# Source and destination rows handled apart, look-ups two groups ahead, codes loaded first

## The reference

```python
def gat_layer(x, W, attn_l, attn_r, bias, src, dst, num_nodes):
    feat = (x @ W).reshape(num_nodes, H, D)
    el = jnp.sum(feat * attn_l[None], axis=-1)
    er = jnp.sum(feat * attn_r[None], axis=-1)
    e = jax.nn.leaky_relu(el[src] + er[dst], NEG_SLOPE)
    ...                                   # softmax over the edges of a destination, weighted sum
edge_index = jnp.stack([src, dst])
x = _layernorm(x + _L0_gnn_ref(x, src, dst, ...))       # two gat layers
x = _layernorm(x + _L1_gnn_ref(x, edge_index, ...))     # mean over the edges
x = _layernorm(x + _L2_gnn_ref(x, edge_index, edge_attr_64, ...))
x = _layernorm(x + _L3_gnn_ref(x, edge_index, ...))     # one attention head
return x
```

## Time and profile before

| | us |
|---|---|
| median of 3 runs | 2458.64 (2457.08 to 2461.86) |
| profiled execution | 2458.36, span 2456.6 |
| busy in the span | PE 1917.6, DVE 1718.3, POOL 1382.8, ACT 1120.3 |
| preparation | 0 to 52.3 |
| first table stage | 52.3 to 537.5 |
| stage b | 537.5 to 763.9 |
| look-up stage | 763.9 to 1050.8 |

### The profile page before, as it was taken

One profiled execution on the slowest core, in us unless ns is written; L12 is line 12 of the kernel. 1 busy time (PEld: TensorE's weight loads), 2 busy tenths in 40 slices (PEclk: granted clock), 3 DMA queues, 4 the chain that ended last, 5 costly groups with the idle time before them and its releaser, 6 DMA issues.

```text
span 2456.6 us, 32122 instructions
## 1 busy us (share of the span) xinstructions
PE 1917.6 (78%) x7888; PEld 1280.3 (52%) x7888; DVE 1718.3 (70%) x6542; ACT 1120.3 (46%) x3061; POOL 1382.8 (56%) x1388
## 2 busy tenths in 40 slices
PE   2998988975877688847756665999995899969883
PEld 2988888864663223236645553666563222235552
DVE  5644444448775876579968986899895566678773
ACT  0322222214665566625535554566664555524332
POOL 5777777730003677700047773477665777727776
PEclk9766666655556788755558886999997555556655
DMA  5655555544224567624449775233531999923340
GB/s 152 191 155 155 155 156 155 155 156 173 105 109 150 171 184 205 183 81 146 151 133 258 212 208 161 93 130 129 166 121 54 335 367 315 305 72 104 127 139 28
DMA packets 272958, 401.94 MB, mean 164 GB/s; under 512 B 98472, under 2 KB 115009, under 8 KB 272645
## 3 DMA queue, kind: packets, MB, share of 16 engines
q1 hardware_dynamic: 215852, 310.35, 38.8%
q0 software_dynamic: 43904, 75.95, 11.7%
q10 hardware_dynamic: 13016, 13.59, 1.6%
HBM read 222.06 MB, written 185.39 MB: 166 GB/s over the span
## 4 chain that ended last, share of the span: by engine, by line
POOL 16%; DVE 13%; issue 11%; ACT 8%; PE 5%; DMA 2%; POOLq 0%; SPq 0%; DVEq 0%; ACTq 0%
POOL ring L667 8%; POOL big L667 4%; POOL out_dram L673 4%; DVE stats L683 3%; ACT outr L729 3%; DVE G L1161 3%; ACT big L1806 2%; DMA ring<-x_t,idx 1%; DVE mv L692 1%; DVE z L1533 1%; DVE z L1876 1%; PE bank L1549 1%; ACT big L1814 1%; PE bank L1545 1%; ACT hT L1792 1%
## 5 line engine op out<-in xcount | busy, mean ns | idle before, releaser
L729 ACT ACTIVATE outr<-z,rn 128x128 f32<-128x128 f32 x784 | 322.7, 483 | 297.1 <-DMA out_dram<-outr,idx 103.7
L667 POOL DMA_INDIRECT ring<-in_x_dram,idx x392 | 379.9, 969 | 137.3 <-issue 118.3
L667 POOL DMA_INDIRECT ring<-x_t,idx x280 | 266.9, 953 | 303.4 <-SPq L303 209.1
L667 POOL DMA_INDIRECT ring<-hidden_e,idx x196 | 195.5, 997 | 309.2 <-DVE idx L1415 251.6
L673 POOL DMA_INDIRECT x_t<-outr,idx x196 | 234.3, 1195 | 160.5 <-ACT outr L729 114.7
L1161 DVE TENSOR_TENSOR_SCAN G<-cont,G,bank 64x512 f32<-64x512 uint8 (+1 forms) x192 | 240.6, 1253 | 35.1 <-PE bank L1239 32.4
L673 POOL DMA_INDIRECT out_dram<-outr,idx x196 | 195.5, 997 | 102.5 <-issue 58.2
L1937 PE MATMUL bank<-DB,z 20*128 20x512 f32 x196 | 201.2, 1128 | 22.8 <-DVE outr L1391 8.1
L1239 PE MATMUL bank<-ident,msg 128*64 128x128 f32 (+1 forms) x588 | 153.2, 415 | 71.4 <-DVE msg L1146 68.5
L1033 DVE BATCH_NORM_STATS2 stats<-ring 128x6 f32<-128x128 f32 x196 | 42.7, 281 | 232.0 <-DMA ring<-in_x_dram,idx 231.8
L1549 PEld LDWEIGHTS bank<-W_s,G 65*128 65x128 f32 (+1 forms) x784 | 165.5, 311 | 65.7 <-issue 63.3
(11 more groups left out here) (384 smaller groups left out, 4548.4 us busy)
## 6 DMA issues: line engine op xcount, KB each, us to landing
hT<-in_x_dram SPq DMA_DIRECT2D x194, 256.0 KB
x_t<-outr SPq DMA_DIRECT2D x98, 256.0 KB
ring<-x_e SPq DMA_DIRECT2D x98, 256.0 KB
x_t<-xload SPq DMA_DIRECT2D x48, 512.0 KB, 3.2
xsrc_e<-ring SPq DMA_DIRECT2D x49, 256.0 KB, 2.8
xd_e<-ring ACTq DMA_DIRECT2D x49, 256.0 KB
ring<-xsrc_e SPq DMA_DIRECT2D x49, 256.0 KB
x_t<-xT SPq DMA_DIRECT2D x49, 256.0 KB
```

What stands on the lines that cost most here:

```text
L667: nc.gpsimd.indirect_dma_start(to(c), None, table, bass.IndirectOffsetOnAxis(ap=idx[:, kind, (g + 1) * GT + c:(g + 1) * GT + c + 1].bitcas ...
L729: ins = nc.scalar.activation(to[:, k, :], frm[:, k, :], ACT.Identity, bias=sc[:, k, 1:2], scale=sc[:, k, 0:1])
```

## The change

Four edits:
- Preparation: ScalarE's two loads of the first indices are issued after its five edge loads and ahead of its weights; VectorE sets the seven constants before it waits for the edges.
- First table stage: the destination rows are counted on a semaphore of their own (`a_to`). Statistics, the store of the source rows and their transposes wait for the source rows only; the transposes and the copies are counted per half (`a_tr`, `a_xT`), and GpSimd waits for each half of a slot apart, the source half without the destination rows' store.
- Look-up stage: `hot`, `look`, `pick` and `hid` run two groups ahead of the rest (`hot` three), the node steps move to groups 8, 17, 26, 35 and 36, to the end of ScalarE's iteration, and ScalarE copies group g - 3 in iteration g instead of g - 1.
- SyncE: the first codes and row loads alternate, four codes instead of three are loaded ahead, and the codes of group g + 4 (before g + 3) are issued in iteration g.

```diff
@@ SHARED (semaphores that the stages share, with their counts)
-            "in": (4, {"a": 2 * GT * 16, "c": GT * 16, "e": GT * 16, "g": GT * 16}),
+            "in": (4, {"a": GT * 16, "c": GT * 16, "e": GT * 16, "g": GT * 16}),
...
-            "tr": (1, {"a": 1, "b": 1, "d": 1, "e": 1, "h": 1}),
+            "tr": (1, {"a": 2, "b": 1, "d": 1, "e": 1, "h": 1}),
@@ prep_loads(eng, half)
                 eng.dma_start(to, frm).then_inc(S("edges"), 16)
+            if half:
+                for n, frm in ((SRC, src), (DST, dst)):
+                    eng.dma_start(idx[:, n, GT:GT + RING * GT], frm[0:RING * GE].rearrange("(c p) -> p c", p=P),
+                                  allow_slow_non_contiguous=True).then_inc(S("idx0"), 16)
             for to, frm in loads[half::2]:
@@ prep_vector(v)
             c.do(v.memset(idx[:, :, GT + NT:], 0))
+            v.wait_ge(S("iotas"), 3)
+            c.do(v.memset(table[:], 0.0))
+            c.do(v.tensor_copy(iota[:], iota_i[:]))
+            c.do(v.tensor_copy(pcol[:], pcol_i[:]))
+            c.do(v.tensor_copy(rc1[:], rc_i[:]))
+            for t in (cross, ecov):
+                c.do(v.memset(t[:, :, CN - 1:CN], 1.0))
+            c.do(v.memset(ecov[:, :, CN - 2:CN - 1], 0.0))
             v.wait_ge(S("shapes"), 8)
...
             v.tensor_copy(hrow[:], bank[4][:, 0:HW]).then_inc(S("hrow"), 1)
-            v.wait_ge(S("iotas"), 3)
-            c.do(v.memset(table[:], 0.0))
...
-            c.do(v.memset(ecov[:, :, CN - 2:CN - 1], 0.0))
             v.wait_ge(S("idx0"), 32)
@@ prep_scalar(a)
-            for n, frm in ((SRC, src), (DST, dst)):
-                a.dma_start(idx[:, n, GT:GT + RING * GT], ...).then_inc(S("idx0"), 16)
             prep_loads(a, 1)
@@ a_pool(pool)
-                need(pool, "a_tr", g + 1 - RING)
+                need(pool, "a_tr", 2 * (g - RING) + 1)
                 need(pool, "a_seen", g + 1 - RING)
-                slot_done(pool, "a_out", i, j, 16, 1)
                 slot_done(pool, "a_src", i, j, 16, 1)
                 gather(pool, lambda c: ring[:, j, 0, c, :], x, SRC, g, S(f"a_in{j}"))
-                gather(pool, lambda c: ring[:, j, 1, c, :], x, DST, g, S(f"a_in{j}"))
+                need(pool, "a_tr", 2 * (g - RING) + 2)
+                slot_done(pool, "a_out", i, j, 16, 1)
+                gather(pool, lambda c: ring[:, j, 1, c, :], x, DST, g, S(f"a_to{j}"))
             at_tiles(step)
+
+        def gathered_dst(eng, g):
+            eng.wait_ge(S(f"a_to{g % RING}"), (g // RING + 1) * GT * 16)
@@ a_sync, a_vector (seen)
-                    gathered(sp, "a", g, 2 * GT * 16)
+                    gathered(sp, "a", g, GT * 16)
@@ a_tensor: turn, project
-                gathered(pe, "a", g, 2 * GT * 16)
-                need(pe, "a_xT", g)
                 for n in range(2):
+                    if n:
+                        gathered_dst(pe, g)
+                    else:
+                        gathered(pe, "a", g, GT * 16)
+                    need(pe, "a_xT", 2 * g - 1 + n)
                     for c in range(GT):
                         ins = nc.tensor.transpose(bank[2 + n][:, c * P:(c + 1) * P], ring[:, g % RING, n, c, :],
                                                   ident[:])
-                ins.then_inc(S("a_tr"), 1)
+                    ins.then_inc(S("a_tr"), 1)
...
-                need(pe, "a_xT", g + 1)
+                need(pe, "a_xT", 2 * g + 2)
@@ a_scalar: columns
-                gathered(a, "a", g, 2 * GT * 16)
-                a.dma_start(edge_row(xd_e, g), ringf[:, j, 1, :]).then_inc(S(f"a_out{j}"), 16)
-                need(a, "a_tr", g + 1)
                 need(a, "a_mm", g - 1)
                 for n in range(2):
-                    ins = nc.scalar.activation(xT[:, s, n, :], bank[2 + n][:], ACT.Copy)
-                ins.then_inc(S("a_xT"), 1)
+                    if n:
+                        gathered_dst(a, g)
+                        a.dma_start(edge_row(xd_e, g), ringf[:, j, 1, :]).then_inc(S(f"a_out{j}"), 16)
+                    need(a, "a_tr", 2 * g + 1 + n)
+                    nc.scalar.activation(xT[:, s, n, :], bank[2 + n][:], ACT.Copy).then_inc(S("a_xT"), 1)
@@ c_tensor
+            for g in range(2):
+                look(g)
             for g in range(NG):
-                look(g)
+                if g + 2 < NG:
+                    look(g + 2)
                 factors(g)
@@ c_vector
+            LEAD = 3
...
-            extra = {9: node[0], 11: node[1], 13: node[2], 15: node[3], 16: scaled}
-            hot(0)
+            extra = {8: node[0], 17: node[1], 26: node[2], 35: node[3], 36: scaled}
+            for n in range(LEAD):
+                hot(n)
+                if n:
+                    pick(n - 1)
+                    hid(n - 1)
             for g in range(NG):
-                if g + 1 < NG:
-                    hot(g + 1)
-                pick(g)
+                if g + LEAD < NG:
+                    hot(g + LEAD)
+                if g + LEAD - 1 < NG:
+                    pick(g + LEAD - 1)
+                    hid(g + LEAD - 1)
                 shifted(g)
-                hid(g)
@@ c_scalar
-            extra = {9: nroot[0], 11: nroot[1], 13: nroot[2], 15: nroot[3]}
+            extra = {8: nroot[0], 17: nroot[1], 26: nroot[2], 35: nroot[3]}
...
-            for g in range(NG + 1):
-                if g in extra:
-                    extra[g]()
+            for g in range(NG + 3):
                 if g < NG:
                     factors(g)
-                if g:
+                if 0 < g <= NG:
                     local(g - 1)
                 if g < NG:
                     apply(g)
-                if g:
-                    copy(g - 1)
+                if g >= 3:
+                    copy(g - 3)
+                if g in extra:
+                    extra[g]()
@@ c_sync
-            for g in range(3):
+            for g in range(4):
                 codes(g)
-            for g in range(2):
-                load(g)
+                if g < 2:
+                    load(g)
             for g in range(NG + 2):
-                if g + 3 < NG:
-                    codes(g + 3)
+                if g + 4 < NG:
+                    codes(g + 4)
```

10 lines of the change are left out of this document (1 added, 9 removed).

## The result

The changed kernel took 2435.02 us (median of four executions, 2433.50 to 2439.09), the kernel before 2457.98 us (four, 2457.08 to 2461.86). The ratio is 0.9904, 95% interval 0.9889 to 0.9920. (Ratios in this text are those of the record; they can differ by up to 0.003 from the quotient of the two medians.) The direction was right and the size too small: 23.0 us instead of 17, at the very end of the stated range (2435 to 2455).

A forecast was written before the change was run, and what follows sets the result against it. The prediction took GpSimd's list of row gathers to bound the first table stage and the look-up stage. 2458.4 - 1.8 - 0.9 - 14.4 = 2441.3, stated as 2441.5 us, 0.7% faster, range 2435 to 2455.

The forecast's parts named there:

- group 4 starts earlier: First table stage: GpSimd starts its fifth group at 61.1 instead of 62.87 us, gain 1.8 (5.5 to a loss of 3).
- 360 gathers: First table stage from group 4 on: still 458 us, 1.273 us a gather, gain 0.
- tail: First table stage, behind the last gather: four of eight transposes already done, gain 0.9 us (0 to 2).
- `b`: The stage between first table stage and look-up stage, 226.4 us: not touched, gain 0.
- start of the look-up stage: Look-up stage, before its first gather: first indices skip an addition, one code load delayed; gain 0.5 us (0.2 to 0.7).
- look-up gathers: Look-up stage, 196 gathers: GpSimd's 16.9 us of waits at node steps go, 3 us of stalls remain.
- Rival 3: Preparation: indices not held up by edge rows, land at 13.5, group 4 at 57; time 2437.5 us; chance 0.08.
- In the steady part the split waits gain nothing: First table stage from group 4 on: split waits free slots asked for only three groups, 30 us, later; gain 0.
- if the time per gather changed: Both stages: 556 gathers at 1.27 to 1.29 us; 0.02 us each are 11 us, making the forecast wrong altogether.
- how many stalls the late copies would leave: Look-up stage: GpSimd waits for ScalarE's copies three groups back; 3 us forecast, 9.8 to 30.5 by rivals.
- Rivals 1 and 2: Look-up stage: copies stall gathers; first, 2448 to 2454 us, chance 0.17; second, slower, 2469 us, chance 0.08.
- Rival 4: First table and look-up stages: waits were hidden, node steps still stall; time within 0.2%; chance 0.07.

The follow-up runs named there:

- e_again: The changed kernel unaltered, run again beside the kernel before: 2443.67 us against 2463.35, ratio 0.9914.
- e_best: Changed kernel with VectorE's bias row in PSUM, look-ups over four banks, first indices loaded first, 97-row loads cut into 96 and 1: 2419.66 us against 2459.47, ratio 0.9835.
- e_split_b: Kernel before with only the first table stage's split edits: 2459.13 us against 2463.35, ratio 0.9977.
- e_seen: Changed kernel, but VectorE's first-stage statistics wait for the destination rows as well: 2441.99 us against 2459.47 for the kernel before, ratio 0.9928.
- e_copy1_b: Changed kernel with ScalarE copying group g - 1 instead of g - 3 in iteration g: 2444.40 us against 2463.35 for the kernel before, ratio 0.9918.
- e_look_b: Kernel before with only the look-up stage's edits: 2443.55 us against 2459.47, ratio 0.9937.
- e_prep: Kernel before with only the preparation's edits, on a chip near 2900 us: 2926.16 us against 2918.97, ratio 1.0015.

## Why the prediction was right in direction and short in size

The two profiles differ by 22.1 us in span. By the steps of the prediction, what it had and what the recorded pair and e_again show (all against the one trace of before):

| step | predicted | recorded | e_again |
|---|---|---|---|
| group 4 starts earlier | 1.8 | 1.4 | 1.3 |
| 360 gathers | 0 | 2.5 | 1.9 |
| tail | 0.9 | 3.1 | 0.9 |
| `b` | 0 | 0 | 0 |
| start of the look-up stage | 0.5 | -0.1 | 0.1 |
| look-up gathers | 13.9 | 14.2 | 13.9 |
| the rest | 0 | 0.9 | -2.6 |
| sum | 17.1 | 22.0 | 15.5 |

*The start came out in time, but in part by luck.* The indices were put at 20.3 and came for a gather at 20.72; the edges at 18.0, 17.44; group 4 at 61.1 without a wait, 61.47. The path of the sum was another one. It let all index packets but one engine's share of 256 pass beside the rows, and 1.9 us of them be left behind these. The packets of ScalarE's queue (q10) from 8 to 10, from 10 to 16 and from 16.1 to 20.5 us:

```profile
q10 hardware_dynamic: 1960, 0.03, 55.2%
...
q10 hardware_dynamic: 72, 0.07, 3.3%
...
q10 hardware_dynamic: 2248, 0.03, 30.1%
```

Most of the first index load passed at 8 to 10, beside the rows. The second load, whose issue lasts from 7.72 to 16.11, brought its packets only after that: all its 2,000 or so waited, where the sum had only the 159 of one engine wait. The 8.39 us of issue stand in no term of the sum. Rival 3 (13.5) is out in its time, though the first load did pass the rows as it said. The step had also taken the 97-row loads as given. With these cut and the indices first, group 4 starts 13.3 us earlier (e_best against the changed kernel), so this part of the change gains 1.4 us and leaves ten times as much behind.

*The failed step is "In the steady part the split waits gain nothing".* The waits indeed gain nothing: the gaps between the 360 gathers make 109.4 to 109.5 us in all ten traces. But the time per gather, which the sum took over unchanged, isn't a constant of GpSimd. It depends on which VectorE operations a gather meets and when, and the split changed that. The 360 gathers take 454.7 to 456.5 us in all eight traces that have it, 457.3 and 458.0 in the two that don't. The prediction had named this as the way to be wrong altogether ("if the time per gather changed") and had given it no range. e_split_b prices the split, steady part and tail together, at 0.9977 (0.9966 to 0.9988), 5.7 us of a kernel of 2460 (4.2 by the medians), where I had 0.9. Its trace against the one of before places 2.1 us in the gathers and 1.3 in the tail; where the rest lies isn't known.

*The tail was right in mechanism, and the recorded 3.1 us are mostly not the change's.* In e_again four of the eight transposes are done before the last rows land, as predicted:

```profile
516.78 1.06 PE L967 MATMUL bank<-ident,ring 128*128 128x128 f32 x4
...
519.84 1.12 PE L967 MATMUL bank<-ident,ring 128*128 128x128 f32 x4 [2.00 <-DMA ring<-in_x_dram,idx]
```

and the tail is 0.9 us shorter, the predicted size. In the recorded trace TensorE is late and turns all eight at once; it saves its time by running the products after them at the full clock, 0.42 us a pair (the granted clock from 519.2 to 525.2 was 0.78; in e_again, from 519.8 to 527.8, 0.50):

```profile
519.22 1.91 PE L967 MATMUL bank<-ident,ring 128*128 128x128 f32 x8
...
522.42 0.34 PE L977 MATMUL bank<-W1x,xT 128*128 128x71 f32 x2
...
522.79 0.42 PE L977 MATMUL bank<-W1x,xT 128*128 128x71 f32 x2
```

where in the kernel before, as in e_again, a pair took 0.68. In six of the seven other traces with the split the tail is 15.4 to 15.8. e_seen has the 16.7 of before: there too all eight are turned at once (at 519.18), but a pair takes 0.68. So it is the clock, and not the split, that makes the recorded tail shorter than predicted; the clock was in no term of the sum.

*The look-up stage came out at the predicted size by two errors.* Forecast and rivals argued over how many stalls the late copies would leave (3 to 30 us). They left none: GpSimd's 16.9 us went whole, 3 more than I had. In exchange the list grew by 2.7 us: 1.5 in the gathers themselves (197.0 against 195.5, 26 long ones instead of 22) and 1.2 in the four usual gaps that stand where the four waits were. The 0.5 us of an earlier start did not come: from the stage's first load to the first gather are 8.7 us, as before. Rivals 1 and 2 are out near 2460 us: e_copy1_b is within 0.1% of e_again. They hold near 2900 us, with their releaser (ScalarE's copy) and their sign. Rival 4 is out by e_look_b.

*And the sum.* e_again's profile is 15.5 us below that of the kernel before, its median 19.7 us below that of the kernel before in its own group. One trace of before carries all differences above, and e_split_b, with the look-up code of the kernel before, waited 22.4 us in that stage and not 16.9. If the kernel before usually waits so, the missing 4 us may be there; the rest of the kernel, untouched by the change, also scatters: from the last look-up gather to the end are 1412.4 to 1416.7 us in these ten traces. No second trace of it near 2460 us was taken, so this is not shown.

## What to carry to other kernels

When GpSimd's list of gathers is the bound, each microsecond beside it counts only by what it does to that list. Compare the time of one gather beside each kind of VectorE operation, and by when the gather starts in it; where it is an operation with two SBUF operands, one of them can go to PSUM. Let the first indices come first. A gain read from one chip's trace belongs to the limit that holds there. The same edits were worth -0.6% where GpSimd issued without waiting and +0.8% where the ring was the limit; the split of the ring's slots gave 0.2% in the one case and 3.5% in the other.

## What the runs showed that I had not expected

- The same kernel takes 2458 to 2463 us on some chips and 2893 to 2922 on others, with nearly equal packet times and a clock of 0.650 against 0.679: in e_prep's first stage 6 of 47 copies that wait for TensorE start 3.3 to 6.2 us late.
- A gather that starts 0.05 to 0.21 us after an addition of two SBUF tensors takes 1.32 to 1.45 us instead of 0.94; with one operand in PSUM it takes 0.94 to 0.95. One that starts earlier or later is hardly longer.
- Cutting three loads of 97 rows into 96 and 1, with the indices first, brought VectorE's first cast of the edges from 17.44 to 8.21 us.
- An issue on ScalarE's queue can itself last long: 8.39 us for the second index load behind five edge loads, 1.08 at the head of the queue.
